# A recurrent layer and a routed expert layer on one core: a 64-column state-space product, and expert jobs issued in halves

## The reference, cut to what matters

```python
def step(carry, inp):                       # 512 times, one after the other
    h_ssm = silu(h_ssm @ A.T + bxt)         # 64 states: the state-space product
    y_ssm = h_ssm @ Cw.T + Cb + dxt
    hh = h_rnn @ W_hh.T + b_hh              # 128 states, gates r, z, n
    r = sigmoid(i_r + h_r); z = sigmoid(i_z + h_z)
    n = tanh(i_n + r * h_n)
    h_rnn = (1.0 - z) * n + z * h_rnn
    y_rnn = h_rnn @ proj_w.T + proj_b
...
for e in range(8):                          # experts, 512 hidden units
    ye = relu(x @ w1[e] + b1[e]) @ w2[e] + b2[e]
    out += where(expert_idx == e, ye * expert_w, 0)
```

## Time and profile before

| | |
|---|---|
| median of 3 runs | 696.96 us |
| the profiled execution | 697.02 us |
| its span | 695.2 us |
| PE busy | 684.6 us (98%) |
| DVE, ACT, POOL busy | 533.8, 429.5, 121.0 us |
| granted TensorE clock | 0.999 |
| units before step 512, in the tail | 440, 218 |

### The profile page before, as it was taken

How to read it: one execution, slowest core, us unless ns; L and a number is a source line. 1 busy time by engine, 2 the same in 40 slices (tenths; PEclk the granted TensorE clock), 3 DMA queues, 4 the chain that set the end, 5 groups by cost and what they waited for, 6 DMA issues and landing times.

```text
span 695.2 us, 35722 instructions
## 1 busy us (share of the span) xinstructions
PE 684.6 (98%) x13868; PEld 641.9 (92%) x13868; DVE 533.8 (77%) x3216; ACT 429.5 (62%) x2688; POOL 121.0 (17%) x209
## 2 busy tenths in 40 slices
PE   7999999999999999999999999999999999999997
PEld 5899999989999999999999999999999999998896
DVE  4777777777887777887887788878877888875666
ACT  4555555556666666557666775676666676666442
POOL 4011111111011111112112211121212212221202
PEclk9999999999999999999999999999999999999999
DMA  8916000603522100044322000642210163323431
GB/s 309 364 61 220 8 7 7 223 33 133 183 94 86 53 15 15 14 168 175 126 86 71 22 15 19 215 163 95 94 61 23 56 230 117 110 67 93 154 102 55
DMA packets 45658, 71.97 MB, mean 104 GB/s; under 512 B 6156, under 2 KB 28498, under 8 KB 45362
## 3 DMA queue, kind: packets, MB, share of 16 engines
q1 hardware_dynamic: 41490, 64.38, 26.3%
q0 software_dynamic: 1984, 4.07, 2.0%
q10 hardware_dynamic: 2016, 1.25, 0.6%
HBM read 14.31 MB, written 21.04 MB: 51 GB/s over the span
## 4 chain that ended last, share of the span: by engine, by line
PE 97%; DVE 1%; issue 0%; ACT 0%; DVEq 0%
PE rs_bank L1223 34%; PE nz_bank L1223 24%; PE hid_bank_b L1223 12%; PE work L1223 11%; PE y_bank L1223 9%; PE hid_bank_a L1223 7%; DVE fin_g L1199 0%; DVE acc L1157 0%; DVE o_sb L1204 0%; DVE hid_b L1179 0%; ACT xT L783 0%; ACT hid_a L790 0%; DVE prob L1023 0%; DVE y_sb L1193 0%; DVE fin_g L1211 0%
## 5 line engine op out<-in xcount | busy, mean ns | idle before, releaser
L1223 PE MATMUL nz_bank<-h_ring,wg 128*64 128x16 f32 x4088 | 207.2, 211 | 0.0
L798 ACT ACTIVATE r_fac<-rs_bank 128x8 f32<-128x8 f32 x512 | 91.6, 179 | 169.0 <-PE rs_bank L1223 161.8
L1223 PE MATMUL rs_bank<-s_ring,ws_sb 128*64 128x128 f32 x1024 | 195.1, 272 | 0.0
L1223 PEld LDWEIGHTS nz_bank<-h_ring,wg 128*64 128x64 f32 x4088 | 160.8, 136 | 1.4
L1223 PE MATMUL rs_bank<-mw,wg 128*64 128x8 f32 x2044 | 146.8, 202 | 0.0
L1223 PE MATMUL rs_bank<-u,wg 128*64 128x8 f32 x2044 | 140.6, 206 | 0.1
L1223 PEld LDWEIGHTS rs_bank<-s_ring,ws_sb 128*64 128x64 f32 x1024 | 127.2, 136 | 9.1
L1104 DVE TENSOR_TENSOR_SCAN nz_bank<-r_fac,nz_bank 128x16 f32<-128x16 f32 x512 | 99.7, 195 | 46.3 <-ACT r_fac L798 30.8
L1108 DVE SCALAR_TENSOR_TENSOR mw<-v_fac,h_ring 128x8 f32<-128x8 f32 x512 | 85.7, 167 | 57.5
L1223 PEld LDWEIGHTS rs_bank<-mw,wg 128*64 128x64 f32 x2044 | 103.4, 135 | 18.8 <-DVE mw L1108 4.6
L804 ACT ACTIVATE v_fac<-nz_bank 128x8 f32<-128x8 f32 x512 | 91.1, 178 | 42.0
(11 more groups left out here) (181 smaller groups left out, 1125.0 us busy)
## 6 DMA issues: line engine op xcount, KB each, us to landing
wx<-w_all SPq DMA_DIRECT2D x58, 578.0 KB, 3.5
rows<-zeros SPq DMA_DIRECT2D x3, 4096.0 KB, 14.5
rows<-y_sb SPq DMA_DIRECT2D x66, 64.0 KB, 1.8
w_all<-in_w SPq DMA_DIRECT2D x2, 2048.0 KB, 15.1
xs_sb<-rows SPq DMA_DIRECT2D x54, 64.0 KB, 2.9
x_sb<-in_x SPq DMA_DIRECT2D x1, 1920.0 KB, 7.4
out<-o_sb SPq DMA_DIRECT2D x19, 64.0 KB, 2.6
out<-o_sb ACTq DMA_DIRECT2D x13, 64.0 KB, 1.7
```

What stands on the lines that cost most here:

```text
L798: nc.scalar.activation(r_fac[:, k, :, 1], r_cols(q, t), ACT.Tanh, scale=0.5).then_inc(rn_ready, 1)
L1223: last = nc.tensor.matmul(out[c:c + COLS], weights[:, c:c + COLS], moving, start=start, stop=stop, skip_group_check=skip_group_check)
```

## The change

`S_WIDE` goes from 128 to 64. The room of a step is counted in halves of 64 columns, five (`HALVES`) in place of four; the tile's work takes two each. A unit that finds room for one half only is begun as the last work of its step, with columns 0 to 63, and ended as the first unit of the next step, with columns 64 to 127 (`BEGUN`). A unit that would begin the sum in `y_bank` (D0) is not split. `hold_clock` fills what is left, up to 320 columns in one product. The groups have 5, 7, 8, 6, 5 tiles, not 6, 7, 7, 6, 5. The tail keeps its three and two units a step.

```diff
-S_WIDE = 128
+S_WIDE = 64
+HALF = 64
-SIZE = [6, 7, 7, 6, 5]
+SIZE = [5, 7, 8, 6, 5]
-ROOM = 2
+HALVES = 5
...
-            place = 0
-            while place < ROOM - taken(u):
+            place = len(at.get(u, []))
+            used = place
+            while used < HALVES - 2 * taken(u):
+                whole = used + 2 <= HALVES - 2 * taken(u)
+                done, spot = (u, place) if whole else (u + 1, 0)
                 for kind in PICK[place > 0]:
                     unit = head[kind][0] if head[kind] else None
-                    where = home(unit, u, place) if unit and ok(unit, u, place, first) else None
-                    if where:
+                    where = home(unit, done, spot) if unit and ok(unit, u, place, first) else None
+                    if where and (whole or unit[0::2] != ("D", 0)):
                         break
...
-                at.setdefault(u, []).append(unit)
-                ready[unit] = (u, place + 1)
+                at.setdefault(done, []).append(unit)
+                if not whole:
+                    begun[u] = unit
+                ready[unit] = (done, spot + 1)
...
-                place += 1
+                place, used = place + 1, used + (2 if whole else 1)
...
+            def unit(kind, i, second, first=0, end=P):
...
+                span = slice(first, end)
+                if first == 0:
+                    wait_for(kind, i, second)
...
-                for kind, n, second in units:
-                    unit(kind, n, second)
+                for i, (kind, n, second) in enumerate(units):
+                    unit(kind, n, second, HALF if i == 0 and g - 1 in BEGUN else 0, P)
+                if g in BEGUN:
+                    unit(*BEGUN[g], 0, HALF)
                 if t == 9:
                     tile_work(c, q, t, g)
                 if exists(c):
-                    room = 0 if g in RELU_OPEN else ROOM - taken(g) - len(units)
-                    if room == 2:
-                        hold_clock(g, len(units), 2 * P)
-                    if room == 1:
-                        hold_clock(g, len(units), P)
+                    room = HALVES - 2 * taken(g) - 2 * len(units) + (g - 1 in BEGUN) - (g in BEGUN)
+                    if room > 0 and g not in RELU_OPEN:
+                        hold_clock(g, len(units), room * HALF)
```

More of the change, by code:

```diff
@@ L237, in schedule @@
                     break
+                if done == NT * T or done in at and not whole:
+                    break
                 head[kind].pop(0)
-                at.setdefault(u, []).append(unit)
-                ready[unit] = (u, place + 1)
+                at.setdefault(done, []).append(unit)
+                if not whole:
+                    begun[u] = unit
+                ready[unit] = (done, spot + 1)
                 if where == "ACT":
-                    act_ops[u + (place > 0)] = act_ops.get(u + (place > 0), 0) + 1
-                    ready[unit] = (u + (place > 0) + 1, 0)
+                    act_ops[done + (spot > 0)] = act_ops.get(done + (spot > 0), 0) + 1
+                    ready[unit] = (done + (spot > 0) + 1, 0)
                     if unit[2]:
@@ L272, in schedule @@
                 on_act.add(what)
-    return at, on_act, relu_open
+    return at, on_act, relu_open, begun
 def pre_steps():
@@ L1342, in unit @@
                 ge(eng, (relu_a_ready, relu_b_ready)[second], 2 * i + h + 1)
[L1343 to L1347, removed]
+            def unit(kind, i, second, first=0, end=P):
+                h = kind in "CB"
+                at = (2 * h + second) * P
+                dense = i in EXPERT_OF
+                e, n = EXPERT_OF.get(i), SLOT_OF.get(i)
+                fixed = None if dense else fixed_expert(n)
+                b = None if dense or fixed is not None else turn(n) % NBUF
+                whole = dense or fixed is not None
+                e = e if dense else fixed
+                span = slice(first, end)
+                if first == 0:
+                    wait_for(kind, i, second)
+                if kind == "X":
+                    source = xs_sb[:, b, :] if n < FIXED0 else xs_last[:, n - FIXED0, :]
+                    last = mm(rows_bank(n)[:, span], source, ident[:, span], start=True, stop=True)
+                    filled = x_filled
+                elif kind in "AC":
+                    last = mm(hid_bank[second][:, span], w_all[:, e, at:at + P] if whole else wx1[:, b, at:at + P],
+                              (h2T[:, (NT - 1) % 2, :] if dense else xT[:, n % 2, :])[:, span], start=True, stop=True)
+                    filled = (w1a_ready, w1b_ready)[second]
+                else:
+                    last = mm((dense_y(e) if dense else y_bank[:, 0:P])[:, span], (hid_a, hid_b)[second][:, h, :],
+                              w_all[:, e, FC * P + at + first:FC * P + at + end] if whole else wx2[:, b, at + first:at + end],
+                              start=kind == "D" and not second, stop=kind == "B" and second > 0 and end == P)
+                    filled = w2_done if second else None
+                if end == P and filled is not None:
+                    last.then_inc(filled, 1)
             def repeated(columns):
```

35 lines of the change are left out of this document (13 added, 22 removed).

## The result

The changed kernel takes 711.51 us in the median (711.05 to 712.1, four runs), the kernel before 697.03 in the same session: a ratio of 1.0213, interval 1.0200 to 1.0226. It is slower by 14.5 us where 4.0 us less were forecast, far outside the range.

What follows compares the result with a forecast made beforehand. The recurrence's chain sets the step (1.207 us), PE close behind; tail units cost full time. Tail -6.4, half pieces +1.2, other loop steps +1.2 sum to -4.0: 693.0 us against 696.96, 8 in 10 for 690.4 to 696.6.

Steps and rivals of the forecast that it cites:

- Other steps of the loop: Loop steps where the new order moves a stall (t = 9, DVE, routing): +1.2 us, good to 1.5 either way.
- The loop eats the gain: Rival: stalls at t = 9, ACT and DVE cost 4 to 5 us, giving 696 to 697; chance 0.17, most or all.
- The clock falls: Rival: 53 emptier steps let PE's clock fall to 1.2 GHz, costing some us, no gain left; chance 0.02.
- slot 54: Tail: its transpose may newly wait for rows loaded after the last scatter, 0 to 1.0 us, most likely 0.3.
- The half pieces: Loop steps with a 64-column piece: 0.006 us longer in about 200 steps, +1.2 us, bounds 0 and +4.0.
- t = 9: Loop steps where PE's transpose waits for h2 (+0.7 us) or a half piece delays ACT's copy (+0.5 us).
- second working of this term: Half pieces by the skill's matmul formula: a piece 0.117 us, a step 0.005 us longer, +1.0 us in all.
- The rival of four weight loads in line: Rival: a half piece costs a whole one, +20 us, 713; called refuted; pieces of 0.14 and worse had 0.05.
- The tail: After step 511: 26 units at 0.257 us move into the loop, -6.4 us, bounds -7.0 and -5.5.

Runs made afterwards that it cites:

- e2: Changed kernel with the n-th of each group's first seven expert loads on SP issued 2n steps later, so stores pass between: 699.62 us, ratio 1.0045.
- e3: Changed kernel with group 2's first gather on POOL at step 462 in place of 453, later gathers moving with it: 699.49 us, ratio 1.0038.
- e5: e1 with a group's first X allowed 6 steps after its expert table is ready, not 4: 696.91 us, ratio 0.9994.
- e10: e2 with the first X of groups 0 and 1 two steps later, new sizes kept: 696.34 us, ratio 0.9996.
- e9: e5 with the 4 MB zeroing of step 32 issued as eight transfers of 0.5 MB: 695.54 us, ratio 0.9974.
- e12: e9 with the first and third zeroing also issued in eight transfers each: 695.51 us, ratio 0.9975.
- e1: Changed kernel with the old group sizes (6, 7, 7, 6, 5), narrow product and half pieces kept: 697.62 us, ratio 1.0002.
- e7: Kernel before with only the new group sizes (5, 7, 8, 6, 5): 707.46 us, ratio 1.0142.
- e11: e7 with SP issuing a group's expert loads only once the last output of the group before is stored: 704.6 us, ratio 1.0117.
- e4: Kernel before with only the state-space product narrowed to 64 columns: 696.56 us, ratio 0.9988.
- e6: e1 with no unit split; an odd half of room is filled by hold_clock with 64 unread columns: 699.28 us, ratio 1.0029.

## Why the prediction was wrong

**"Other steps of the loop" is the part that failed.** It summed +1.2 us, "good to 1.5 either way", and went through PE, ACT and DVE. It did not follow SP and POOL for group 2: its last outputs nine steps earlier, two steps behind group 3's six loads, and its first gather nine steps earlier. The order showed both, and the trace of before SP's pace, 2.8 to 2.9 us a load. The missing terms are +8.65 (the wait) and +4.2 (the lower clock behind it), shown by e2 and e3. "The loop eats the gain" was priced as some 20 small delays; one large one did it. "The clock falls" named emptier steps as the cause; it fell behind a stall.

**The first X** of a group (112, 224) was also missed: +2.2, shown by e5 and e10. I checked such a load only for slot 54.

**Steps 18 and 44**, +1.4: nothing in the forecast stood for them. That the large transfers cause them is shown by e9 and e12, and that what comes late behind them is PE's own instructions by the packets of q8. The Trainium skill, "Runtime: NRT & Kernel Launch", section Instruction fetch mechanics, says that each sequencer fetches its instructions in 16 KiB blocks through a DMA queue of its own, mostly hidden. The trace agrees on the blocks (three transfers, 0.05 MB, in the 21 us above); the waits of 0.36 and 0.77 us are cases where it was not hidden.

**The half pieces** were sized right in mechanism: the product at 0.70, the next step 0.51 to 0.52 later. The median full step becomes 0.010 to 0.012 longer, not 0.006, which would be 2.0 to 2.4 us for 200 of them. Summed step by step against before, t = 9 and 14 and the named steps left out, they add 1.3 us in the changed kernel and 2.1 to 2.2 in e5, e9, e10 and e12, where 1.2 were forecast: some of these steps had lost time before. The prediction's second working of this term, a half piece of 0.117 us, has a slip: the narrow product is then 0.117 as well, and the two are 0.010 over a whole pass of 0.223, not 0.005, so it would have given +2.0 and not +1.0. The rival of four weight loads in line is refuted: a piece takes 0.11 us, and "TensorE: Matmul & The Clock Gate" (the Trainium skill, section LDWEIGHTS), whose 53 ns a load make 0.21 for four in line, holds here only if loads overlap.

**t = 9** came as said in the steps that were named: 201 and 313 at 1.41 and 1.43 (said 1.40), 137 and 409 at 1.34 and 1.35 (said 1.34). All steps at t = 9 but 457 add 1.7 us, where 1.2 were forecast; those at t = 14 but 462 add 0.6, which no term stood for.

**The tail** gave 5.1, not 6.4, in the changed kernel and 4.2 to 5.5 in e1, e5, e9, e10 and e12. 26 units at 0.257 us are right (6.7); what is missing are 1.6 us of waits, chiefly DVE's `y_sb` behind tile 31's routing. I had looked for a new wait at slot 54 only, and there the changed kernel has none.

With the avoidable meetings taken out (e5 and e10), the change is worth -0.2 to -0.5 us, inside what can be told from none: the tail gives 5.5 and 4.8, and the fifth half, t = 9 and 14 and the large transfers take nearly all of it back.

## What to carry to other kernels

When an order of work moves, follow each queue that it passes, SP's and POOL's first: who is behind the moved wait on that engine, up to the critical path. A store that shares a queue with a burst of loads is late by the whole burst, and here moving the waiting gather cured it as well as moving the burst. Look at the first use of each thing that such a burst loads, and split a transfer of megabytes that is in no hurry: the fetch of instructions has to pass it.

## What the runs showed of the hardware

- A stall costs more than its length. Behind 7.95 us of idle time PE had the lower clock for five steps, 4.2 us; behind 4.83 us (e7) it cost about 2.5, and behind 2.15 us (e11) two steps of 1.97 and 1.90, some 1.4. Waits of 1.0 us in the tail of the changed kernel brought no drop.
- A transfer of 4 MB can hold up PE for 0.4 to 0.9 us with no semaphore to show for it, because a 16 KB block of PE's instructions lands late behind it; in eight parts of 512 KB over 28 steps it did not.
- A float32 product of 64 columns takes 0.11 us of PE's stream and one of 128 columns 0.22, both with four records: with 64 columns the pace is still that of the columns.
- Freeing 0.11 us of PE in a full step shortened it by nothing (e4), while filling it again lengthened it by 0.01 (e6): PE and the recurrence's chain are that close.
